# The value products of four attention layers as one product of 1120 columns in three parts a token half

## The chip, the cores and the metric

The kernel runs on one core of a Trainium2 chip. The metric is the device time of one execution in microseconds (us); lower is better. Everything is float32.

## What is computed

Four cross-attention layers follow each other on 128 sequences of 64 tokens and 128 channels. All four read the same context of 64 tokens and 256 channels per sequence. Layer 0 has 16 heads of 64; layers 1 to 3 have 16 query heads of 8 that share 4 key and value heads. Cut to what matters:

```python
# layer 0: x (128, 64, 128), ctx (128, 64, 256)
q = x @ Wq; k = ctx @ Wk; v = ctx @ Wv            # Wv: (256, 1024)
logits = einsum('bhqd,bhkd->bhqk', q, k) * 64 ** -0.5 + col_bias
x = einsum('bhqk,bhkd->bhqd', softmax(logits), v) @ Wo + bo + x
# layers 1 to 3, n_rep = 4
xn = x * rsqrt(mean(x * x) + 1e-5) * norm_w
q = xn @ wq; k = ctx @ wk; v = ctx @ wv           # wv: (256, 32)
scores = einsum('bgrtd,bsgd->bgrts', q, k) / sqrt(8)
x = x + einsum('bgrts,bsgd->btgrd', softmax(scores), v) @ wo
```

The values of all four layers are products of the same context with 1024 + 3 x 32 = 1120 columns of weights.

## The kernel before

**Tiling.** The batch is cut into 32 groups of four sequences (G = 4, so 256 tokens, in two token halves of 128, NP = 2). A group goes through these steps; the names are those of the tables and of the code.

- cT: transpose of the context. k (four units, 256 columns x four blocks): keys of layer 0. v (four units): values of layer 0, unit u for token half u // 2 and column half u % 2, a product of 512 columns with two parts of the contraction. k3: keys of the small layers. v3: values of the small layers, 96 columns for each token half, both in one bank.
- xT: transpose of x, q0 (four units): queries of layer 0. s: scores. add, max, sub, exp, sum, rcp, nrm: the softmax, four units of [128, 512] a layer. t: transposes of the probabilities on TensorE, et: their copy back on ScalarE. pv0, wo0: probabilities times values and the output product of layer 0.
- For layers 1 to 3: xt, q, s, the softmax, t and et, pv, wo, and x2, ssq, ms for the root mean square.

In this text t1.0 is unit 0 of step t of layer 1, v5 is unit 5 of v, and a step without a layer number belongs to layer 0 (t.2, et.0).

**Every float32 product is two instructions** in the trace, each with its own weight load, so a v step of two matmul calls shows as four.

**The order** is written out. Tables (PE_TIME, ACT_TIME, DVE_TIME, POOL_TIME, SP_TIME, lines 38 to 115) give each step a slot for group 0; group g comes PERIOD = 44.42 later. `steps` (L123) sorts the slots, and only the order of the result is used: each engine runs its steps one after the other and waits by semaphore for what a step needs. Steps of several groups so lie interleaved: while group g is at s of layer 0, group g-1 is in layers 1 and 2, group g-2 in layer 3, and keys and values of g+1 and g+2 are made.

**The banks.** PSUM has four banks for scores and four for all else. The latter are dealt in turn, in the order of TensorE's steps (L239 to 246), one to a step, two to pv0, none to s. Before TensorE writes a bank, it waits for the engine that empties the step that held it (L386 to 392): for a t step that is et on ScalarE, for most others ScalarE too, for wo0 and wo VectorE. So a step waits until the step four places before it is emptied.

**Buffers that this touches:** V (three, values of layer 0), VB (five, values of the small layers, laid out in a zeroed 48-column pattern so that one product serves all heads). A v bank is emptied by one copy of 512 columns (L550), the v3 bank by four copies of 64 partitions x 96 (L558).

**The start.** SP's queue issues the loads (L284 to L306): context of groups 0 and 1, Wk and Wv in two halves each, x of group 0, context of group 2, Wq, then per small layer wk, wv, wq, wo and the norm, then bo and Wo. `l_sm` counts the small ones, and its last value is awaited in one go. Ahead of the products of a k step TensorE runs 12 or 13 waits on a semaphore that has long been met (PE_FILL, L403).

Of the kernel before, what the change touches and what calls it, by code (L numbers as in the profile page):

```python
# [29 lines left out]

# [4 lines left out]
PE_FILL = (13, 12, 12, 12)  # L36
PERIOD = 44.42
PE_TIME = {
    "cT": {0: (0,)},
    "k": {0: (87.13, 53.5, 69.79, 100.51)},  # L40
    "v": {0: (76.65, 104.7, 93.39, 95.33)},
    "k3": {0: (106.87,)},
    "v3": {0: (119.52,)},
    "xT": {0: (104.43,)},
    "q0": {0: (127.22, 128.52, 123.66, 130.25)},
    "s": {0: (135.84, 134.86), 1: (170.09,), 2: (201.09,), 3: (235.6,)},
    "t": {0: (152.37, 152.81, 153.25, 154.12),
          1: (185.9, 186.33, 188.92, 181.8),
          2: (216.93, 219.96, 218.23, 218.66),
          3: (256.06, 253.91, 246.56, 247.05)},  # L50
    "pv0": {0: (154.65, 155.64)},
    "wo0": {0: (160.36,)},
    "xt": {1: (164.84,), 2: (196.58,), 3: (228.38,)},
    "q": {1: (167.65,), 2: (198.11,), 3: (232.91,)},
    "pv": {1: (192.23,), 2: (222.65,), 3: (257.89,)},
    "wo": {1: (195.27,), 2: (225.72,), 3: (259.99,)},
}
ACT_TIME = {
    "cT": {0: (1.97,)},
    "k": {0: (89.05, 55.41, 73.19, 105.46)},  # L60
    "v": {0: (79.49, 106.67, 95.3, 97.24)},
    "k3": {0: (107.93,)},
    "v3": {0: (120.61,)},
    "xT": {0: (104.9,)},
    "q0": {0: (128.28, 129.57, 127.42, 131.77)},
    "exp": {0: (146.18, 140.23, 145.62, 141.07),
            1: (177.19, 178.4, 180.19, 174.99),
            2: (210.83, 213.91, 205.74, 205.03),
            3: (247.73, 244.1, 239.23, 240.44)},
    "et": {0: (153.01, 153.5, 153.99, 154.76),  # L70
           1: (186.59, 187.08, 189.55, 182.94),
           2: (217.62, 221.12, 218.92, 220.13),
           3: (256.7, 254.76, 247.24, 248.45)},
    "pv0": {0: (156.34, 157.32)},
    "x2": {1: (169.12,), 2: (200.39,), 3: (226.99,)},
    "xt": {1: (165.63,), 2: (197.14,), 3: (229.63,)},
    "q": {1: (168.84,), 2: (198.9,), 3: (233.61,)},
    "pv": {1: (194.03,), 2: (223.8,), 3: (259.05,)},
}
DVE_TIME = {  # L80
    "add": {0: (140.99, 136.97, 140.1, 136.04)},
    "max": {0: (142.36, 138.07, 141.68, 138.75),
            1: (172.53, 175.26, 173.9, 171.24),
            2: (206.32, 203.59, 202.91, 202.23),
            3: (242.1, 240.75, 236.75, 237.43)},
    "sum": {0: (147.03, 143.03, 146.35, 143.99),
            1: (178.19, 179.29, 183.85, 176.63),
            2: (212.11, 214.8, 210.55, 208.98),
            3: (250.07, 245.23, 241.42, 243.67)},
    "rcp": {0: (149.94, 143.79, 150.14, 145.07),  # L90
            1: (178.95, 181.15, 185.21, 177.99),
            2: (214.49, 216.34, 211.91, 210.35),
            3: (251.42, 246.32, 242.78, 245.03)},
    "wo0": {0: (164.14,)},
    "ssq": {1: (169.66,), 2: (201.49,), 3: (233.51,)},
    "sub": {1: (174.57, 177.3, 175.94, 173.21),
            2: (209.66, 211.22, 204.95, 204.26),
            3: (244.34, 242.98, 238.1, 239.19)},
    "wo": {1: (195.91,), 2: (226.51,), 3: (260.97,)},
}  # L100
POOL_TIME = {
    "xb": {0: (129.82,)},
    "sub": {0: (143.48, 138.82, 142.43, 139.87)},
    "nrm": {0: (150.22, 144.52, 151.26, 145.57),
            1: (179.31, 181.43, 185.49, 178.27),
            2: (214.77, 216.62, 212.19, 210.62),
            3: (251.7, 247.4, 243.05, 245.31)},
    "ms": {1: (173.24,), 2: (201.97,), 3: (235.46,)},
}
SP_TIME = {  # L110
    "cT": {0: (114.98,)},
    "kr": {1: (126.98,), 2: (115.48,), 3: (147.9,)},
    "xT": {0: (215.32,)},
    "st": {0: (292.17,)},
# [4 lines left out]
ON_ACT = ("xT", "q0", "pv0", "xt", "q", "pv", "cT", "k", "v", "v3", "k3")  # L119
# [36 lines left out]
def xattn_kernel(nc, t):  # L156
    with ExitStack() as ctx:
# [16 lines left out]
        wv0 = sb("wv0", [128, 2, 1024])  # L174
# [5 lines left out]
        wvs = sb("wvs", [128, 2, 3, 32])  # L180
# [70 lines left out]
        l_wk, l_wv = ([signal(f"{n}{i}", [i], 16) for i in range(2)] for n in ("l_wk", "l_wv"))  # L251
        l_sm = signal("l_sm", range(17), 16)
# [29 lines left out]
        def sync_program(e):  # L282
# [7 lines left out]
            for i, half in enumerate(halves):  # L290
                e.dma_start(wv0[:, :, half], wv_r[:, :, half]).then_inc(l_wv[i].sem, 16)
# [39 lines left out]
        def gpsimd_program(e):  # L331
# [9 lines left out]
            w.wait_ge(l_sm, 16)  # L341
# [26 lines left out]
        def tensor_program(e):  # L368
# [9 lines left out]
            for st in PE_ORDER:  # L378
# [21 lines left out]
                elif kind == "k":  # L400
                    w.wait_ge(a_ev, ("cT", g, 0, 0))
                    w.wait_ge(l_wk[u // 2], u // 2)
                    for _ in range(PE_FILL[u]):  # L403
                        e.wait_ge(l_ident.sem, 16)
# [6 lines left out]
                elif kind == "v":  # L411
# [346 lines left out]
```

## Time and profile before

| | |
|---|---|
| median of 3 runs | 1492.88 us (1490.64 to 1494.28) |
| profiled execution | time 1492.95 us, span 1491.0 us |
| TensorE busy (products) | 1449.9 us, 97% |
| TensorE busy (weight loads) | 1161.2 us, 78% |
| VectorE busy | 1087.8 us, 73% |
| ScalarE busy | 1038.8 us, 70% |
| GpSimd busy | 774.4 us, 52% |
| mean granted clock of TensorE | 0.987 of 2.4 GHz |

The span is the time from the first to the last instruction; the time of the execution is 1.95 us longer. Busy time of TensorE is from a product's start to its modelled end, and the ends overlap the next start by some 0.16 us; what a step costs TensorE is therefore read as the distance from its start to the start of the next.

### The profile page before, as it was taken

To read this page: it belongs to the slowest core of one execution; us is meant where nothing else is said; L and a number is where in the kernel's file an instruction comes from. 1 tells how busy PE (TensorE), PEld (TensorE's weight loads), DVE (VectorE), ACT (ScalarE), POOL (GpSimd) and SP (SyncE) were. 2 spreads that over 40 slices of the span, in tenths; PEclk is the share of its full clock that TensorE was granted. 3 is DMA by queue.
4 is the path that set the end of the run, shared out by engine and by line. 5 is a ranking of instruction groups with operands and counts; after the bars stand their busy time and mean duration, and the time that the engine had idled before them with its cause. 6 is when DMAs were issued, how large, how long until landed. Compare 5 with 4: busy or idle time off the path is not lost.

```text
span 1491.0 us, 56683 instructions
## 1 busy us (share of the span) xinstructions
PE 1449.9 (97%) x23872; PEld 1161.2 (78%) x23872; DVE 1087.8 (73%) x2291; ACT 1038.8 (70%) x2145; POOL 774.4 (52%) x881
## 2 busy tenths in 40 slices
PE   8999999999999999999999999999999999999875
PEld 5777877887877887877887877887877887877664
DVE  1467777777777877777777777777777777777874
ACT  3566776776776776776777776777776777777663
POOL 3345555545555545555545555545555545555642
PEclk9999999999999999999999999999999999999986
DMA  5010100110000111000110000111000110000000
GB/s 146 21 24 19 26 14 25 27 26 25 22 14 25 27 26 25 21 15 25 26 27 24 22 16 24 26 27 24 22 19 20 26 27 25 15 17 16 15 11 8
DMA packets 57178, 36.94 MB, mean 25 GB/s; under 512 B 16864, under 2 KB 55776, under 8 KB 56928
## 3 DMA queue, kind: packets, MB, share of 16 engines
q1 hardware_dynamic: 56032, 33.22, 8.8%
q8 instruction: 192, 3.15, 0.9%
q14 instruction: 58, 0.48, 0.1%
q10 hardware_dynamic: 896, 0.10, 0.0%
HBM read 16.49 MB, written 4.19 MB: 14 GB/s over the span
## 4 chain that ended last, share of the span: by engine, by line
PE 95%; DVE 2%; ACT 1%; SPq 1%; issue 1%; ACTq 0%; POOL 0%; DMA 0%; POOLq 0%; DVEq 0%
PE bank L408 15%; PE bank L474 15%; PE bank L416 15%; PE bank L492 7%; PE bank L443 7%; PE scores L465 7%; PE bank L511 7%; PE scores L454 4%; PE bank L483 4%; PE bank L517 4%; PE bank L373 3%; PE bank L498 3%; PE bank L424 2%; PE bank L431 2%; SPq L323 1%; DVE st L672 1%
## 5 line engine op out<-in xcount | busy, mean ns | idle before, releaser
L357 POOL TENSOR_TENSOR E<-E,st 128x512 f32<-128x512 f32 x512 | 531.7, 1044 | 609.5 <-DVE st L684 600.2
L681 DVE TENSOR_REDUCE st<-E 128x8 f32<-128x512 f32 x512 | 342.3, 674 | 119.2 <-ACT E L585 64.6
L593 ACT COPY E<-bank 128x512 f32<-128x512 f32 x512 | 290.3, 589 | 30.6 <-PE bank L474 29.6
L474 PEld LDWEIGHTS bank<-ident,E 128*128 128x128 f32 x2048 | 242.4, 143 | 75.1 <-issue 42.8
L672 DVE TENSOR_REDUCE st<-scores 128x8 f32<-128x512 f32 x384 | 254.3, 684 | 63.2 <-PE scores L465 63.2
L474 PE MATMUL bank<-ident,E 128*128 128x128 f32 x2048 | 289.8, 278 | 10.4 <-POOL E L357 10.4
L589 ACT ACTIVATE E<-E,inv 128x512 f32<-128x512 f32 x384 | 277.1, 730 | 23.3 <-DVE E L676 22.4
L676 DVE TENSOR_TENSOR E<-scores,st 128x512 f32<-128x512 f32 x384 | 256.1, 674 | 0.0
L408 PE MATMUL bank<-cT,wk 128*128 128x256 f32 x1024 | 244.8, 383 | 2.1 <-ACT cT L539 1.9
L416 PE MATMUL bank<-wv,cT 128*128 128x512 f32 x512 | 240.5, 593 | 0.0
L408 PEld LDWEIGHTS bank<-cT,wk 128*128 128x128 f32 x1024 | 187.3, 192 | 25.4 <-ACT cT L539 2.3
L353 POOL TENSOR_TENSOR E<-E,st 128x512 f32<-128x512 f32 x128 | 130.9, 1044 | 39.1 <-DVE st L669 39.1
L416 PEld LDWEIGHTS bank<-wv,cT 128*128 128x128 f32 x512 | 87.6, 190 | 62.7 <-issue 62.6
L443 PE MATMUL bank<-xT,wq 128*128 128x256 f32 x512 | 131.0, 380 | 0.0
L511 PEld LDWEIGHTS bank<-E,VB 128*32 128x32 f32 x6144 | 92.7, 112 | 35.7 <-issue 17.4
L492 PEld LDWEIGHTS bank<-wo,QT 128*128 128x128 f32 x1024 | 119.2, 192 | 1.6
L492 PE MATMUL bank<-wo,QT 128*128 128x128 f32 x1024 | 119.5, 275 | 0.0
L580 ACT ACTIVATE QT<-bank 128x512 f32<-128x512 f32 x128 | 77.1, 603 | 57.1 <-PE bank L517 37.2
L662 DVE TENSOR_TENSOR E<-scores,bias 128x512 f32<-128x512 f32 x128 | 86.6, 677 | 40.7 <-PE scores L454 37.1
L511 PE MATMUL bank<-E,VB 128*32 128x64 f32 x6144 | 108.4, 223 | 6.5 <-ACT E L593 6.4
L465 PE MATMUL scores<-KB,QT 32*64 32x256 f32 x3072 | 109.2, 392 | 4.3 <-issue 2.2
L544 ACT COPY KT<-bank 128x512 f32<-128x512 f32 x128 | 74.9, 585 | 46.0 <-PE bank L408 42.0
(62 smaller groups left out, 1689.6 us busy)
## 6 DMA issues: line engine op xcount, KB each, us to landing
KB<-K SPq DMA_DIRECT2D x1536, 8.0 KB
cin<-in_ctx SPq DMA_DIRECT2D x32, 256.0 KB, 2.9
xin<-in_x SPq DMA_DIRECT2D x32, 128.0 KB, 2.5
out<-xN SPq DMA_DIRECT2D x32, 128.0 KB, 1.9
wk<-in_L_xattn_Wk SPq DMA_DIRECT2D x2, 512.0 KB, 7.8
wv<-in_L_xattn_Wv SPq DMA_DIRECT2D x2, 512.0 KB, 9.7
wq<-in_L_xattn_Wq SPq DMA_DIRECT2D x1, 512.0 KB, 9.4
wo<-in_L_xattn_Wo SPq DMA_DIRECT2D x1, 512.0 KB, 5.3
```

Of the source, the lines that this page charges most:

```text
L357: e.tensor_tensor(E3, E3, wide(stat[s][u][:, 16:24]), ALU.mult).then_inc(g_nrm.sem, 1)
L408: m = e.matmul(bank[:, T * jj:T * jj + T], wk0[:, k, 128 * j:128 * j + 128], cTg[:, k, :], start=(k == 0), stop=(k == 1))
L416: m = e.matmul(bank[:, :], cTg[:, k, 128 * p:128 * p + 128], wv0[:, k, 512 * half:512 * half + 512], start=(k == 0), stop=(k == 1))
L443: m = e.matmul(bank[:, T * jj:T * jj + T], wq0[:, 128 * j:128 * j + 128], xT[s][:, :], start=True, stop=True)
L474: m = e.transpose(bank[:, 128 * k:128 * k + 128], E[s][u][:, 128 * k:128 * k + 128], ident[:, :])
L492: m = e.matmul(bank[:, 128 * p:128 * p + 128], QT[s][:, j, 128 * p:128 * p + 128], wo0[:, j, :], start=(j == 0), stop=(j == 7))
L511: m = e.matmul(bank[32 * r:32 * r + 32, 64 * b:64 * b + 64], VBg[:, b, c:c + 32], E[s][2 * (b // 2) + r // 2][:, n:n + 64], start=(gp == 0 ...
L589: e.activation(E[s][u][:, :], E[s][u][:, :], ACT.Exp, scale=inv[s][:, u // 2:u // 2 + 1]).then_inc(a_exp.sem, 1)
L593: e.copy(E[s][u][:, :], bank_of["t", g, l, u][:, :]).then_inc(a_et.sem, 1)
L672: e.tensor_reduce(stat[s][u][:, 0:8].rearrange("p (r h) -> p r h", r=2), scores_of[g, l, u], AX, ALU.max).then_inc(d_max.sem, 1)
L676: e.tensor_tensor(pairs(E[s][u][:, :]), scores_of[g, l, u], stat[s][u][:, 0:8].rearrange("p (r h a) -> p r h a", r=2, a=1).to_broadcast([1 ...
L681: e.tensor_reduce(stat[s][u][:, 8:16], heads(E[s][u][:, :]), AX, ALU.add).then_inc(d_sum.sem, 1)
```

## The change

A new table `VCOLS` cuts the 1120 columns (1024 of layer 0 and 3 x 32) into 374, 374 and 372. The weights lie in one buffer `wv` of 1120 columns. Step v now has six units, unit u for token half u // 3 and column part u % 3; v3 is gone. Parts 0 and 1 are emptied by one copy of 374 columns each. Part 2 is emptied by a copy of the 276 columns that belong to layer 0 and by four copies of 64 partitions x 48 into VB.

The loads of the value weights change: the two parts of 374 columns, then the 276 columns and the three small matrices, all ahead of x of group 0, with a semaphore `l_wvs` of their own. pv0 waits for all three parts of its token half, pv for units 2 and 5. The empty waits ahead of k are left out for group 0. All five tables have new slots, and PERIOD is 44.18.

The core of the diff:

```diff
+VCOLS = ((0, 374), (374, 748), (748, 1120))
-PERIOD = 44.42
+PERIOD = 44.18
 PE_TIME = {
-    "k": {0: (87.13, 53.5, 69.79, 100.51)},
-    "v": {0: (76.65, 104.7, 93.39, 95.33)},
-    "v3": {0: (119.52,)},
-    "s": {0: (135.84, 134.86), 1: (170.09,), 2: (201.09,), 3: (235.6,)},
-          1: (185.9, 186.33, 188.92, 181.8),
-    "q": {1: (167.65,), 2: (198.11,), 3: (232.91,)},
+    "k": {0: (96.87, 67.67, 82.19, 116.05)},
+    "v": {0: (89.47, 99.45, 117.77, 107.38, 105.68, 108.86)},
+    "s": {0: (146.31, 147.29), 1: (180.68,), 2: (213.22,), 3: (246.23,)},
+          1: (198.49, 199.79, 198.93, 193.56),
+    "q": {1: (179.1,), 2: (210.24,), 3: (243.55,)},
 ACT_TIME = {
-    "v": {0: (79.49, 106.67, 95.3, 97.24)},
-    "v3": {0: (120.61,)},
-    "et": ... 1: (186.59, 187.08, 189.55, 182.94),
+    "v": {0: (92.68, 103.53, 119.22, 108.83, 107.13, 110.31)},
+    "et": ... 1: (199.48, 200.76, 200.27, 195.89),
 SP_TIME = {
-    "cT": {0: (114.98,)},
-    "st": {0: (292.17,)},
+    "cT": {0: (104.14,)},
+    "st": {0: (281.38,)},
...
-        wv0 = sb("wv0", [128, 2, 1024])
-        wvs = sb("wvs", [128, 2, 3, 32])
+        wv = sb("wv", [128, 2, 1120])
...
-            for i, half in enumerate(halves):
-                e.dma_start(wv0[:, :, half], wv_r[:, :, half]).then_inc(l_wv[i].sem, 16)
+            for i, (lo, hi) in enumerate(VCOLS[:2]):
+                e.dma_start(wv[:, :, lo:hi], wv_r[:, :, lo:hi]).then_inc(l_wv[i].sem, 16)
+            e.dma_start(wv[:, :, 748:1024], wv_r[:, :, 748:1024]).then_inc(l_wvs.sem, 16)
+            for l in range(3):
+                e.dma_start(wv[:, :, 1024 + 32 * l:1056 + 32 * l], t[f"L{l + 1}_xattn_wv"].rearrange(
+                    "(k p) n -> p k n", p=128)).then_inc(l_wvs.sem, 16)
             e.dma_start(xin[0][:, :, :], x_r[0]).then_inc(l_x[0].sem, 16)
             e.dma_start(cin[2][:, :, :], c_r[2]).then_inc(l_c[2].sem, 16)
...
-                    for _ in range(PE_FILL[u]):
+                    for _ in range(PE_FILL[u] if g else 0):
                         e.wait_ge(l_ident.sem, 16)
...
                 elif kind == "v":
                     w.wait_ge(a_ev, ("cT", g, 0, 0))
-                    p, half = u // 2, u % 2
-                    w.wait_ge(l_wv[half], half)
+                    p, i = u // 3, u % 3
+                    lo, hi = VCOLS[i]
+                    if i < 2:
+                        w.wait_ge(l_wv[i], i)
+                    else:
+                        w.wait_ge(l_wvs, 3)
                     for k in range(2):
-                        m = e.matmul(bank[:, :], cTg[:, k, 128 * p:128 * p + 128],
-                                     wv0[:, k, 512 * half:512 * half + 512], start=(k == 0), stop=(k == 1))
-                    m.then_inc(p_ev.sem, 1)
-                elif kind == "v3":
-                    w.wait_ge(a_ev, ("cT", g, 0, 0))
-                    w.wait_ge(l_sm, 16)
-                    for p in range(NP):
-                        for k in range(2):
-                            m = e.matmul(bank[:, 96 * p:96 * p + 96], cTg[:, k, 128 * p:128 * p + 128],
-                                         wvs[:, k, :, :].rearrange("p l n -> p (l n)"), start=(k == 0), stop=(k == 1))
+                        m = e.matmul(bank[:, 0:hi - lo], cTg[:, k, 128 * p:128 * p + 128], wv[:, k, lo:hi],
+                                     start=(k == 0), stop=(k == 1))
                     m.then_inc(p_ev.sem, 1)
...
                 elif kind == "v":
                     w.wait_ge(p_ev, st)
+                    p, i = u // 3, u % 3
+                    lo, hi = VCOLS[i]
                     if g >= NV:
                         w.wait_ge(p_ev, ("pv0", g - NV, 0, 0), ("pv0", g - NV, 0, 1))
-                    e.copy(V[g % NV][:, u // 2, 512 * (u % 2):512 * (u % 2) + 512], bank[:, :]).then_inc(a_ev.sem, 1)
-                elif kind == "v3":
-                    w.wait_ge(p_ev, st)
-                    w.wait_ge(g_zero, NVB - 1)
-                    if g >= NVB:
-                        w.wait_ge(p_ev, ("pv", g - NVB, 3, 0))
-                    for g2 in range(2):
-                        for b2 in range(2):
-                            m = e.copy(
-                                VB[g % NVB][64 * g2:64 * g2 + 64, :, :].rearrange(
-                                    "q (p b) (i c) -> q p b i c", b=2, c=48)[:, :, b2, :, 8 * g2:8 * g2 + 8],
-                                bank[64 * b2:64 * b2 + 64, 0:96 * NP].rearrange(
-                                    "q (p i g d) -> q p i g d", p=NP, i=6, g=2)[:, :, :, g2, :])
+                    m = e.copy(V[g % NV][:, p, lo:min(hi, 1024)], bank[:, 0:min(hi, 1024) - lo])
+                    if i == 2:
+                        w.wait_ge(g_zero, NVB - 1)
+                        if g >= NVB:
+                            w.wait_ge(p_ev, ("pv", g - NVB, 3, 0))
+                        for g2 in range(2):
+                            for b2 in range(2):
+                                m = e.copy(
+                                    VB[g % NVB][64 * g2:64 * g2 + 64, 2 * p + b2, :].rearrange(
+                                        "q (i c) -> q i c", c=48)[:, :, 8 * g2:8 * g2 + 8],
+                                    bank[64 * b2:64 * b2 + 64, 1024 - lo:1120 - lo].rearrange(
+                                        "q (i g d) -> q i g d", i=6, g=2)[:, :, g2, :])
                     m.then_inc(a_ev.sem, 1)
```

By the slots, the parts of a beat that matter below run in this order on the two engines (the number in brackets is the group, relative to that of s). TensorE, before: s(0), s(0), wo2(-2), t1.3(-1), v2(+1), xt3(-2), v3-unit(+1), t1.0(-1), t1.1(-1), k1(+2). TensorE, after: s(0), s(0), pv2(-2), t1.3(-1), v4(+1), wo2(-2), v3-unit(+1), xt3(-2), v5(+1), t1.0(-1), t1.2(-1), q3(-2), t1.1(-1), k1(+2), s3(-2), and later v2(+1), wo1(-1), t.0(0), k3(+1), xt2(-1), t.1(0), t.2(0). ScalarE, after: v3-unit(+1), exp.0, xt3, v5, et1.0, q3, et1.2, et1.1, exp.1, and later v2, et.0, k3, xt2, et.1. ("v3-unit" is unit 3 of step v.) At the start TensorE's order is cT, cT(1), k1, k2, v0, k0, cT(2) before, and cT, cT(1), k1, k2, cT(2), v0, k0 after.

## Rows read from the trace of the kernel before

**Rows 1.** The page, part 1: busy us (share of the span), instructions.
```profile
span 1491.0 us, 56683 instructions
PE 1449.9 (97%) x23872; PEld 1161.2 (78%) x23872; DVE 1087.8 (73%) x2291; ACT 1038.8 (70%) x2145; POOL 774.4 (52%) x881
```

**Rows 2.** Busy time of each engine in a stretch (window, its length, busy us).
```profile
190.00:1000.00 810.00, 809.94 (x13559) 651.12 (x13558) 615.78 (x1291) 586.96 (x1219) 433.32 (x491) 1.00 0.09 23
```

**Rows 3.** The chain that ended last, in order of time: start us, us, what.
```profile
36.94 1.73 PE bank L408 x8
...
55.00 0.09 issue
55.09 1.97 PE bank L408 x8
...
131.38 2.10 PE bank L483 x128
...
1290.54 2.09 PE bank L483 x128
```

**Rows 4.** TensorE's timeline, 631 to 636 us: start us, us, instruction, count.
```profile
631.10 1.03 PE L424 MATMUL bank<-wvs,cT 128*128 128x96 f32 x8
631.96 0.38 PE L373 MATMUL bank<-ident,xN 128*128 128x128 f32 x2
632.18 0.60 PE L474 MATMUL bank<-ident,E 128*128 128x128 f32 x4
632.62 1.88 PE L416 MATMUL bank<-wv,cT 128*128 128x512 f32 x4
634.34 0.60 PE L474 MATMUL bank<-ident,E 128*128 128x128 f32 x4
634.77 0.60 PE L498 MATMUL bank<-xT,wqs 128*128 128x256 f32 x2
635.21 1.03 PE L443 MATMUL bank<-xT,wq 128*128 128x256 f32 x4
```

**Rows 5.** The same timeline, around two steps "wo", at 638 and 662 us.
```profile
638.25 0.71 PE L517 MATMUL bank<-wos,QT 128*128 128x128 f32 x4
638.79 1.03 PE L443 MATMUL bank<-xT,wq 128*128 128x256 f32 x4
...
662.50 0.61 PE L517 MATMUL bank<-wos,QT 128*128 128x128 f32 x4
662.95 1.03 PE L431 MATMUL bank<-cT,wks 128*96 128x256 f32 x4
```

**Rows 6.** ScalarE's timeline, 632 to 634 us.
```profile
632.16 0.97 ACT L558 COPY VB<-bank 64x96 f32<-64x96 f32 x4 [2.80 <-PE bank L424]
633.16 0.37 ACT L611 COPY xT<-bank 128x256 f32<-128x256 f32 x1
633.43 0.59 ACT L593 COPY E<-bank 128x512 f32<-128x512 f32 x1
```

**Rows 7.** ScalarE's groups by line: busy us, mean ns of one, idle before.
```profile
L550 ACT COPY V<-bank 128x512 f32<-128x512 f32 x128 | 75.1, 587 | 35.6 <-PE bank L416 34.8
L558 ACT COPY VB<-bank 64x96 f32<-64x96 f32 x128 | 29.9, 234 | 87.0 <-PE bank L424 85.9
```

**Rows 8.** Timeline of SP's queue at 6 us.
```profile
6.22 0.53 SPq L293 DMA_DIRECT2D cin<-in_ctx  x1
```

**Rows 9.** The tile cin between 6 and 18 us: its one load.
```profile
DMA to landing us min/median/max: 8.5/8.5/8.5
```

**Rows 10.** TensorE's timeline at the start, 15 to 19 us.
```profile
15.41 1.88 PE L416 MATMUL bank<-wv,cT 128*128 128x512 f32 x4
...
18.86 0.60 PE L373 MATMUL bank<-ident,cin 128*128 128x128 f32 x4
```

**Rows 11.** TensorE's timeline near the end: s of layer 0, last group.
```profile
1398.42 1.26 PE L454 MATMUL scores<-KT,QT 64*64 64x64 f32 x68
```

More of the change, by code:

```diff
@@ L74 @@
[L74 to L78, printed above, removed]
+    "cT": {0: (1.57,)},
+    "k": {0: (99.25, 71.97, 84.11, 117.97)},
+    "v": {0: (92.68, 103.53, 119.22, 108.83, 107.13, 110.31)},
+    "k3": {0: (120.97,)},
+    "xT": {0: (116.66,)},
+    "q0": {0: (142.23, 143.94, 139.53, 140.39)},
+    "exp": {0: (153.41, 157.06, 157.62, 158.18),
+            1: (190.7, 192.3, 185.7, 186.91),
+            2: (225.63, 220.28, 218.71, 224.19),
+            3: (258.05, 259.75, 256.35, 251.03)},
@@ L79 @@
+    "et": {0: (164.29, 165.81, 166.3, 167.12),
+           1: (199.48, 200.76, 200.27, 195.89),
+           2: (235.6, 234.39, 226.6, 233.9),
+           3: (265.32, 267.22, 261.36, 261.85)},
+    "pv0": {0: (168.69, 170.39)},
+    "x2": {1: (179.34,), 2: (211.79,), 3: (240.62,)},
+    "xt": {1: (178.03,), 2: (209.71,), 3: (242.34,)},
+    "q": {1: (179.72,), 2: (210.98,), 3: (244.17,)},
+    "pv": {1: (204.25,), 2: (237.85,), 3: (269.15,)},
 }
 DVE_TIME = {
-    "add": {0: (140.99, 136.97, 140.1, 136.04)},
@@ L82 @@
[L82 to L99, printed above, removed]
+    "add": {0: (148.07, 148.96, 152.37, 153.74)},
+    "max": {0: (149.65, 153.06, 154.43, 156.19),
+            1: (181.83, 188.76, 183.38, 184.26),
+            2: (218.84, 214.36, 216.39, 215.04),
+            3: (252.64, 255.37, 249.96, 247.52)},
@@ new lines @@
+    "sum": {0: (155.52, 157.79, 158.47, 160.02),
+            1: (191.58, 194.52, 187.41, 188.09),
+            2: (226.89, 223.37, 221.8, 225.07),
+            3: (259.9, 261.46, 257.23, 254.7)},
+    "rcp": {0: (156.87, 159.82, 161.39, 162.27),
+            1: (192.95, 196.36, 190.33, 189.44),
+            2: (228.24, 224.47, 223.17, 226.69),
+            3: (261.26, 262.82, 258.32, 256.05)},
+    "wo0": {0: (176.5,)},
+    "ssq": {1: (179.88,), 2: (213.72,), 3: (243.48,)},
+    "sub": {1: (186.72, 189.64, 184.93, 185.62),
+            2: (221.11, 219.51, 217.95, 222.48),
+            3: (254.01, 256.25, 253.32, 249.07)},
@@ L100 @@
+    "wo": {1: (208.04,), 2: (240.14,), 3: (274.68,)},
 }
 POOL_TIME = {
[L102 to L108, printed above, removed]
+    "xb": {0: (147.62,)},
+    "sub": {0: (150.4, 153.81, 155.18, 156.94)},
+    "nrm": {0: (158.99, 160.1, 161.67, 162.71),
+            1: (193.23, 196.64, 190.76, 189.72),
+            2: (228.52, 224.75, 223.44, 226.96),
+            3: (261.53, 263.1, 258.6, 256.32)},
@@ L250, in xattn_kernel @@
         l_wq = signal("l_wq", ["l_wq"], 16)
-        l_wk, l_wv = ([signal(f"{n}{i}", [i], 16) for i in range(2)] for n in ("l_wk", "l_wv"))
-        l_sm = signal("l_sm", range(17), 16)
+        l_wk = [signal(f"l_wk{i}", [i], 16) for i in range(2)]
+        l_wv = [signal(f"l_wv{i}", [i], 16) for i in range(2)]
+        l_wvs = signal("l_wvs", range(4), 16)
+        l_sm = signal("l_sm", range(14), 16)
         l_b = signal("l_b", range(7), 16)
@@ L477, in tensor_program @@
                     w.wait_ge(a_et, ("et", g, 0, 2 * u), ("et", g, 0, 2 * u + 1))
-                    w.wait_ge(a_ev, ("v", g, 0, 2 * u), ("v", g, 0, 2 * u + 1))
+                    w.wait_ge(a_ev, *[("v", g, 0, 3 * u + i) for i in range(3)])
                     for j in range(8):
@@ L537, in scalar_program @@
                     if g >= NC:
-                        w.wait_ge(p_ev, ("v3", g - NC, 0, 0), ("k3", g - NC, 0, 0), *[(k, g - NC, 0, i) for k in "kv" for i in range(4)])
+                        w.wait_ge(p_ev, ("k3", g - NC, 0, 0), *[("k", g - NC, 0, i) for i in range(4)],
+                                  *[("v", g - NC, 0, i) for i in range(6)])
                     e.copy(cT[g % NC][:, :, :].rearrange("p k n -> p (k n)"), bank[:, :]).then_inc(a_ev.sem, 1)
```

53 lines of the change are left out of this document (20 added, 33 removed).

## The prediction

> **What bounds the kernel now.** I read the page first: TensorE is busy 97% of the span [rows 1]. Then the stretches: from 190 to 1000 us it is busy 809.94 of 810 us [rows 2], so in the middle nothing but the sum of its steps counts, and an idle tenth in every group would be paid about 30 times. The chain in order of time gives the beat: product P·V of layer 0 comes at 131.38 us and, 26 groups later, at 1290.54, which is 44.583 us for a group of four batches [rows 3]. ScalarE has room on average (70%), but an average doesn't tell whether one particular copy is in time, and that is what the case turns on.
>
> TensorE's own timeline prices the steps, start to next start [rows 4]. A "v" step (512 columns, four instructions) takes 1.72 us (632.62 to 634.34), so 0.430 an instruction. A "k" step (256 columns, eight instructions) takes 1.73 by the chain (the piece at 36.94) [rows 3], so 0.216. The "v3" step (96 columns, eight instructions) takes 0.86 (631.10 to 631.96), so 0.108: far more than its share by columns (96/512 of 0.430 is 0.081), since each of its instructions brings a new load of 128 weight columns. That is what the change goes for.
>
> **The products.** Before, a group has four v steps and one v3: 4 x 1.72 + 0.86 = 7.74 us, 24 instructions. After, it has six v steps of 374, 374 and 372 columns, again 24 instructions. The trace has none of that width. Between the 256 and the 512 columns of [rows 3, 4] a line gives 0.216 + 118/256 x 0.214 = 0.315 for 374 and 0.313 for 372, so 16 x 0.315 + 8 x 0.313 = 7.54. Gain 0.20 us a group. If the neighbours' rounding is wrong by 2 ns an instruction it is 0.15 to 0.25. The weight load lies under a 0.315 us product as it does under the 0.216 us one. For 32 groups: -6.5 us (-4.8 to -8.0).
>
> **The order around narrow products.** Steps on 32 or 64 rows or columns of the array ("s", "pv", "pv0") form four runs in a group, before and after by the two tables. Leaving such a run costs the next step: "wo" after s1 takes 0.54 (638.25 to 638.79), "wo" after a v step 0.45 (662.50 to 662.95) [rows 5]. In the new order wo2 and wo3 no longer follow a run (-0.18), two "t" steps do instead (nothing to +0.09 each), and a t step rather than cT stands ahead of s0 (nothing to +0.07). Between -0.18 and +0.07; the planner's own slots for these five steps come to -0.04, which lies near the middle, and I take it: -1.3 us in 32 groups (-5.8 to +2.2).
>
> **The copies on ScalarE, and the new wait.** In place of one v3 step whose bank was emptied by four copies of 64 x 96, two steps in a group (v2 and v5, the third part of each token half) must be emptied by one copy of 276 columns and four of 64 x 48. As work this is little: before, 4 x 0.587 + 4 x 0.234 = 3.3 us [rows 7]; after, 4 copies of 374 columns, 2 of 276 and 8 small ones, some 4.2 us; one more in 44. As a delay it is not little. What is seen: a copy of 256 columns lasts 0.37 and the next starts 0.27 after it (633.16, 633.43), so wide copies overlap by 0.10. The four small ones don't: four take 0.97 with 0.234 for one [rows 7], so they start 0.245 apart (one duration and 0.011), and the copy behind them starts at 633.16, 0.03 after their end [rows 6]. A 64 x 48 copy has 48 columns less, at (0.589 - 0.37)/256 = 0.86 ns a column 0.04 us: 0.194, spaced 0.205. The 276-column copy lasts 0.37 + 0.017 = 0.387; I give it no overlap with the small one behind it, as none is seen in the other direction (with overlap 0.10 less). So the bank of v5 is emptied in 0.40 + 3 x 0.205 + 0.194 = 1.21 us. The table of the change sets the next ScalarE step, et1.0, only 0.81 us behind v5.
>
> Who waits: the banks are dealt in turn, four of them. After v5 TensorE runs t1.0, t1.2, q3, t1.1, k1. So t1.1 needs the bank of v5, and k1 the bank of t1.0, which et1.0 empties, and et1.0 stands behind v5's copies in ScalarE's queue. TensorE has t1.0, t1.2, q3 and t1.1 to do before k1: four steps of 0.43 to 0.44 (a t at 632.18, a q at 634.77), 1.74 us [rows 4]. ScalarE's side, from the same instant: 0.20 until its first copy starts (631.96 to 632.16), 1.21 for the bank, 0.03 to the next, 0.59 for et1.0, and about 0.09 until a k step runs after a copy that it waited for (the "issue" piece at 55.00) [rows 3, 6]: 2.12 us. TensorE stands for 0.38 us in every group, some 0.2 of it already ahead of t1.1. With the first copy overlapped it is 0.27; with small copies still 0.245 apart, 0.53. This happens where v5, layer 1's transposes and a further group's k1 all exist, 30 times: +11.4 us (+8 to +16). Queued behind the wait on TensorE are only k1, s3 and all that follows in its order; ScalarE isn't made late by it. The same five copies after v2 fit: xt2, which takes that bank, comes 0.44 + 0.44 + 0.86 = 1.74 later against 0.20 + 1.21 + 0.09 = 1.50, and t.2, which needs et.0's bank, comes 0.22 + 0.44 later still.
>
> The Trainium skill ("ScalarE: Activation LUTs", section "What ACT_TABLE_LOAD costs") says that back-to-back ACTIVATEs overlap by about 93 ns. The wide copies of [rows 6] agree (0.10), the four narrow ones don't. By the page the bank would be free about 0.5 us sooner and the wait would be gone; that is the first rival below.
>
> **The start.** Four transfers of value weights (the 276 columns, and three small ones that stood among the small weights) now go ahead of x of group 0, the context of group 2 and Wq in SP's queue. That context was issued at 6.22 and landed 8.5 later, at 14.7; an issue there costs 0.53 [rows 8, 9], so it lands 0.5 to 2.1 later. The new order wants it two steps sooner: not at 18.86, behind v0 and k0, but at 15.4, right behind the first two k steps [rows 10]. A wait of nothing to 1.5 us; I take 0.8. The rest of the moved transfers is covered: x is wanted some 10 us later. The 12 or 13 empty waits ahead of each k step, gone in group 0, cost at most 0.1. In the first groups the reordered softmax steps of layer 0 are nearer to their consumers; nothing to 2, I take 0.5. In the steady part SP's queue keeps its 48 small copies a group; by the new slots it issues its loads 23 and 28 us ahead of the steps that want them, and the store 28 us ahead: nothing.
>
> **The end.** From s0 of the last group at 1398.42 [rows 11] to 1491 us the chain runs through four layers with TensorE often idle. By both tables the same steps of the two groups before it are left at that point but for pv2, 1 us of TensorE's; the order within DVE's and GpSimd's steps differs. The wait for an old store, which was level with the Wo product there, goes. I put nothing, with 4 either way.
>
> **Sum**, against the profiled execution (span 1491.0, time 1492.95, 0.07 above the median of the runs): -6.5 - 1.3 + 11.4 + 0.8 + 0.5 = +4.9. So 1492.9 + 4.9 = 1497.8 us, and a beat of 44.58 - 0.20 - 0.04 + 0.38 = 44.72.
>
> **Rivals.** (1) The narrow copies overlap after all, or the bank is free earlier for another reason: no wait at t1.1 and k1, the beat is 44.34, and the time 1497.8 - 11.4 = 1486.4, faster. For it: wide copies overlap, and the table was laid out with 0.81 us. Against it: the same kind of copy in the trace takes 0.245 where the old table allowed 0.15, and there the bank was wanted only 2 us later, so that nothing showed. The point from which it decides: v5's bank emptied and et1.0 begun within about 0.86 us. (2) The wait is there at half the size (first copy overlapped and the lag to k1 shorter): 0.2 a group, 6 us, 1492.4, no difference. (3) A column costs more at widths that aren't a power of two, or the wide step does not pay: no gain of 0.20, with the wait, 1504. (4) The new order waits in further places at the start and the end, or for the copies of v2 too: 5 us and more on top, 1503.
>
> **How the numbers follow.** Chances: forecast 0.55, spread by the bounds of the wait over 1494 to 1503; rival 1 0.26; rival 2 0.11; rivals 3 and 4 together 0.08. The range 1485.5 to 1503 takes in rival 1 but for the part of it where the order's gain too is large, and leaves out about 0.15. A measurement tells 0.3%, 4.5 us, from nothing: faster is below 1488.4, slower above 1497.4. Rival 1 is nearly all faster (0.26). Of the forecast 0.35 lies above 1497.4 and of the last two 0.07: slower 0.42. The rest is the same, 0.32.
>
> **What would show it.** In the changed kernel's profile: matmuls of 374 columns spaced 0.315; no step of 96 columns; the beat of P·V at 44.72. TensorE idle 30 times by some 0.2 ahead of a transpose, released by a copy into V or VB, and 30 times by some 0.2 ahead of K, released by a copy into E. ScalarE's five copies lasting 1.2 us in all. A wait for the context near 15 us. Wrong would be: small copies spaced 0.1, a middle without idle time (then 1486), a wait elsewhere, or more than 5 us of difference in the last 90 us.

## Result and the profile after

| | before | after |
|---|---|---|
| median, measured on the same chip | 1491.76 us (4 runs) | 1525.3 us (4 runs, 1517.76 to 1533.28) |
| ratio after / before | | 1.0225, 95% interval 1.0156 to 1.0293 |
| profiled execution | 1492.95 us, span 1491.0 | 1533.28 us, span 1531.4 |

The changed kernel is 33.5 us slower. The forecast was 1497.8 us, at most 1503; the time lies outside that range. The page of after, with its queue of instruction loads:

```profile
span 1531.4 us, 56792 instructions
PE 1464.2 (96%) x23872; PEld 1189.2 (78%) x23872; DVE 1071.4 (70%) x2291; ACT 1077.0 (70%) x2337; POOL 776.7 (51%) x881
...
q8 instruction: 192, 3.15, 0.9%
```

ScalarE has 192 more instructions and 38 us more of work [rows 1]. TensorE's busy time grew by 14 us, though its products should have become shorter. Its waits, summed (engine, line, what it waited for: us in total, times, longest):

```profile
PE bank L485 <- issue: 26.7, 15, 2.4
PE bank L476 <- POOL E L363: 10.7, 8, 6.4
```

L485 is P·V of layer 0 (pv0). In 15 of 32 groups TensorE stops in the middle of this step, and no wait on another engine ends then: "issue" is time in which the profile shows nothing that it waited for. The wait on GpSimd is that of the last groups, where before has 10.4 us of the same. One such stop in the timeline (start, us, instruction, count), and the windows around it (length, then busy us of PE, PEld, DVE, ACT and POOL, the granted clock, DMA share, GB/s):

```profile
133.41 1.59 PE L485 MATMUL bank<-E,V 64*64 64x64 f32 x90
137.12 1.10 PE L485 MATMUL bank<-E,V 64*64 64x64 f32 x38 [2.12 <-issue]
138.15 2.01 PE L467 MATMUL scores<-KB,QT 32*64 32x256 f32 x32
```

```profile
134.00:137.00 3.00, 1.00 (x66) 0.86 (x57) 1.49 (x4) 2.59 (x6) 1.63 (x2) 1.00 0.09 18
137.10:141.00 3.90, 3.88 (x75) 2.70 (x76) 0.74 (x2) 1.69 (x3) 1.03 (x3) 0.56 0.07 15
141.00:145.00 4.00, 4.00 (x30) 3.75 (x30) 4.00 (x9) 2.13 (x4) 1.85 (x2) 1.00 0.06 12
```

After 90 of 128 products nothing runs for 2.12 us. Behind it the granted clock is 0.56: TensorE falls to the lower of its two levels, 1.2 GHz, for most of 3.9 us, and step s that follows takes 2.01 us for the usual 1.05. Such a beat is 48.6 to 48.8 us long, and there are four. Of the eight stops of 2.1 us and more a fifth, ending at 1376.06, is followed by 0.56 as well, but lies in the last groups, where beats are shorter. The other three leave the clock at 1.00, and their beats are 46.6 to 47.1.

Where no stop falls, the kernel does what was forecast. The same stretch as [rows 4], TensorE and then ScalarE:

```profile
629.83 1.42 PE L426 MATMUL bank<-wv,cT 128*128 128x372 f32 x4
631.09 1.04 PE L476 MATMUL bank<-ident,E 128*128 128x128 f32 x8
631.96 0.60 PE L500 MATMUL bank<-xT,wqs 128*128 128x256 f32 x2
632.43 0.66 PE L476 MATMUL bank<-ident,E 128*128 128x128 f32 x4
633.07 1.97 PE L414 MATMUL bank<-cT,wk 128*128 128x256 f32 x8
634.97 1.12 PE L467 MATMUL scores<-KB,QT 32*64 32x256 f32 x32
```

```profile
631.29 0.39 ACT L555 COPY V<-bank 128x276 f32<-128x276 f32 x1 [0.21 <-PE bank L426]
631.57 0.81 ACT L562 COPY VB<-bank 64x48 f32<-64x48 f32 x4
632.40 0.58 ACT L597 COPY E<-bank 128x512 f32<-128x512 f32 x1
```

v5 takes 1.26 us (629.83 to 631.09). The five copies end at 632.38, and t1.1, which needs their bank, comes only 0.05 later, at 632.43; et1.0 ends at 632.98, and k1 comes at 633.07. The products carry no bracket for these waits, since modelled ends overlap the next start. In the distances they are seen: from q3 to t1.1 it is 0.47 for a usual 0.43, from t1.1 to k1 0.64 for 0.44, k1 takes 1.90 for 1.82. The weight loads, which come just ahead of the products, do show them, summed over the run (engine, line, what it waited for: us in total, times, longest):

```profile
PEld bank L476 <- ACT VB L562: 8.0, 29, 0.3
PEld bank L414 <- ACT E L597: 5.6, 28, 0.2
```

These are the two signs that the prediction had named: some 0.2 to 0.3 us behind a copy into VB, and 0.2 behind a copy into E, in nearly every group. The beat of this group is 44.71 us, pv0 at 599.62 to pv0 at 644.33.

**Where the 40.4 us between the two spans lie.** pv0 of group 2 comes 2.0 us later than in before (133.41, 131.38). From there to pv0 of the last group it is 1323.4 us instead of 1284.7: 38.7 more. The rest is 0.4 shorter. Of the 38.7 some 3.8 are the longer beat of clean groups (29 x 0.13), 26.7 the stops, and some 9 the half clock behind five of them (beats of 48.6 against 46.8, so 1.8 each). The three make 39.5; before has a stop of 1.37 us in the same stretch, near 1401, so they account for 38.1.

### The profile page after: what moved, and what is told of

It is laid out like the page before. It is cut to its first block, busy times and chain, and to the rows that moved or that the text cites. A ratio compares the mean times of both kernels' runs of the same rounds, so it can differ in the third digit from the quotient of the medians.

```text
span 1531.4 us, 56792 instructions
## 1 busy us (share of the span) xinstructions
PE 1464.2 (96%) x23872; PEld 1189.2 (78%) x23872; DVE 1071.4 (70%) x2291; ACT 1077.0 (70%) x2337; POOL 776.7 (51%) x881
## 3 DMA queue, kind: packets, MB, share of 16 engines
q8 instruction: 192, 3.15, 0.9%
## 4 chain that ended last, share of the span: by engine, by line
PE 93%; DVE 3%; issue 2%; ACT 1%; SPq 1%; DMA 0%; POOL 0%
PE bank L426 16%; PE bank L476 15%; PE bank L414 15%; PE bank L445 7%; PE bank L494 7%; PE scores L467 7%; PE bank L513 7%; PE bank L485 5%; PE scores L456 4%; PE bank L379 3%; PE bank L519 3%; PE bank L500 3%; PE bank L433 2%; DVE st L676 1%; DVE E L680 1%
## 5 line engine op out<-in xcount | busy, mean ns | idle before, releaser
L685 DVE TENSOR_REDUCE st<-E 128x8 f32<-128x512 f32 x512 | 336.3, 667 | 153.4 <-ACT E L593 99.4
L476 PE MATMUL bank<-ident,E 128*128 128x128 f32 x2048 | 301.1, 282 | 10.9 <-POOL E L363 10.7
L476 PEld LDWEIGHTS bank<-ident,E 128*128 128x128 f32 x2048 | 239.1, 144 | 76.0 <-POOL E L363 24.6
L426 PE MATMUL bank<-wv,cT 128*128 128x374 f32 (+1 forms) x768 | 271.5, 477 | 0.0
L414 PE MATMUL bank<-cT,wk 128*128 128x256 f32 x1024 | 248.7, 386 | 1.3 <-ACT cT L542 1.0
L426 PEld LDWEIGHTS bank<-wv,cT 128*128 128x128 f32 x768 | 136.5, 190 | 52.5
L555 ACT COPY V<-bank 128x374 f32<-128x374 f32 (+1 forms) x192 | 86.0, 448 | 74.8 <-PE bank L426 73.4
L445 PE MATMUL bank<-xT,wq 128*128 128x256 f32 x512 | 125.8, 380 | 0.0
L699 DVE TENSOR_TENSOR xN<-bank,xN 128x256 f32<-128x256 f32 x96 | 40.3, 420 | 120.6 <-PE bank L519 120.6
L467 PE MATMUL scores<-KB,QT 32*64 32x256 f32 x3072 | 113.1, 402 | 4.9 <-issue 2.6
```

What stands on the lines that cost most here:

```text
L414: m = e.matmul(bank[:, T * jj:T * jj + T], wk0[:, k, 128 * j:128 * j + 128], cTg[:, k, :], start=(k == 0), stop=(k == 1))
L426: m = e.matmul(bank[:, 0:hi - lo], cTg[:, k, 128 * p:128 * p + 128], wv[:, k, lo:hi], start=(k == 0), stop=(k == 1))
L445: m = e.matmul(bank[:, T * jj:T * jj + T], wq0[:, 128 * j:128 * j + 128], xT[s][:, :], start=True, stop=True)
L476: m = e.transpose(bank[:, 128 * k:128 * k + 128], E[s][u][:, 128 * k:128 * k + 128], ident[:, :])
L685: e.tensor_reduce(stat[s][u][:, 8:16], heads(E[s][u][:, :]), AX, ALU.add).then_inc(d_sum.sem, 1)
```

## Experiments

Three questions: what causes the stops, whether the wait behind the five copies is real and of the forecast size, and whether another order does better. In this part the *place* of an instruction is its number in TensorE's program, modulo 256. In both kernels a group has exactly 1536 instructions, six pieces, so from group 3 on each step keeps its place. pv0 stands at 19 in before and at 13 in after.

### The empty waits

```diff
-                    for _ in range(PE_FILL[u] if g else 0):
+                    for _ in range(PE_FILL[u]):
```

> The changed kernel with one line of the change undone: the empty waits ahead of each k step run in group 0 too, which puts 25 more instructions ahead of everything that follows on TensorE and changes nothing else. Theory A (the 16 standstills of some 2 us inside pv0 are instructions that come late, and come late because of where in the 16 KB pieces of the instruction stream pv0 lies, at place 13 of 256): they go or move, the beat is 44.71 in all groups, time about 1496. Theory B (they come from the new order or the wider products themselves, whatever the place): they stay, time 1515 to 1533. If both places are bad, pv0 (now 38) and s0 (now 36) stand still elsewhere, and the text of A has to say so.

Measured: 1497.65 us (1496.39 to 1499.41), ratio 1.0041 [1.0026, 1.0055]. The stops in pv0 are gone but for two, in group 1 and in group 30, 3.4 us together; the beat is 44.62, in some groups 44.72 to 44.82. One line that adds 25 instructions to group 0 is worth 27.7 us. pv0 now stands at 38.

The other way round, the same line in the kernel before:

```diff
-                    for _ in range(PE_FILL[u]):
+                    for _ in range(PE_FILL[u] if g else 0):
```

> The kernel before with only the one line of the change that leaves the empty waits out in group 0: 25 instructions less, pv0 at place 250 instead of 19, s0 at 131 instead of 156. Theory A: standstills may appear somewhere, 1495 to 1530, with the beat 44.58 where there is none. Theory B: nothing happens, 1492.

1492.67 us, ratio 1.0002 [0.9993, 1.0012], beat 44.58. The waits in group 0 have no use of their own, and the old order bears this shift. Is place 13 for pv0 bad in itself? The kernel before with `PE_FILL[u] if g or u != 1 else 0` has pv0 there:

> The kernel before with 6 instructions less on TensorE in group 0: pv0 at place 13, where the changed kernel has it, all else as before (s0 at 150). Theory A in its simple form (the place of pv0 decides): standstills in pv0, 1505 to 1530. Theory B: 1492.

1491.59 us, ratio 0.9997 [0.9987, 1.0007]. It isn't. And the changed kernel with pv0 at the place that it has in before, 19 (`PE_FILL[u] if g else (12 if u == 1 else 0)`):

> The changed kernel with 6 more instructions on TensorE in group 0 (12 empty waits ahead of its k1), so that pv0 lies at place 19 of a piece in the steady part, exactly where it lies in the kernel before, and s0 at 17. Theory A: if the place of pv0 alone decides, no standstill, 1496. If what counts is how the place meets the waits ahead of pv0, standstills may stay: 1510 to 1530. Theory B: 1515 to 1533.

1532.93 us, ratio 1.0273 [1.0240, 1.0307], 15 stops of 27.6 us. So place 19 serves the old order and not the new one. The remaining question was whether e1 helps by the place or by slowing the start. 50 empty waits ahead of k1 of group 0 alone (`50 if u == 1`), 25 instructions in one spot:

> The changed kernel with 50 empty waits ahead of k1 of group 0 alone, 25 instructions: pv0 and s0 at places 38 and 36 as in e1, but not spread over four k steps. Place alone: like e1, 1497 to 1499. If it counts that the waits stand ahead of each k step of group 0, the standstills are back, 1515 to 1533.

1499.95 us, ratio 1.0047 [1.0032, 1.0062], beat 44.62, and no stop in pv0 between groups 2 and 29. The count decides, not which steps have the waits.

### Half a piece further

256 empty waits, 128 instructions, ahead of k1 of group 0, in the new order (`256 if u == 1 else 0`) and in the old one (`PE_FILL[u] + (0 if g or u != 1 else 256)`):

> The changed kernel with 256 empty waits ahead of k1 of group 0, which are 128 instructions: pv0 at place 141 and s0 at 139, half a piece further. Theory A (the place decides): no standstill in pv0 or s0 at this place, beat 44.6 to 44.7, 1498 and at most 1 more for the waits. If instead half a piece is bad as well, standstills in other steps, over 1510. Theory B (leaving out the waits is bad for another reason than place): since waits are there again, this tells nothing against A.

> The kernel before with 256 further empty waits ahead of k1 of group 0, 128 instructions: pv0 at place 147 and s0 at 28. If the old order too has places at which instructions come late, standstills in pv, s or s0 and 1500 to 1590 (e7 gave 1589 for the new order at such a place). If the old order is safe everywhere (it was at 250, 13 and 19), 1493 to 1505, some 13 at most for the piece that the waits themselves want at the start.

1589.47 us, ratio 1.0648 [1.0622, 1.0674], and 1559.32 us, ratio 1.0446 [1.0428, 1.0465]. So the old order isn't immune. The stops lie in other steps now; waits of the two kernels:

```profile
PE bank L513 <- issue: 39.8, 29, 2.6
PE scores L467 <- issue: 18.2, 32, 1.2
PE bank L414 <- issue: 12.8, 1, 12.8
```

```profile
PE scores L465 <- issue: 19.2, 31, 1.2
PE scores L454 <- issue: 13.9, 26, 1.2
PE bank L408 <- issue: 13.5, 1, 13.5
```

Then the better variant (below) with the waits of group 0 doubled, pv0 at 62:

```diff
-                    for _ in range(PE_FILL[u]):
+                    for _ in range(PE_FILL[u] * (1 if g else 2)):
```

> As e13 with twice as many empty waits in group 0, so 24 more instructions: pv0 at place 62, s0 at 60. If only places just behind the start of a piece are bad, as e13. e7 at 141 was bad, so somewhere between 38 and 141 the standstills in pv and s begin: if at 62 already, over 1500.

1513.93 us, ratio 1.0139 [1.0125, 1.0153], 27 stops in t. One stop of each of the three kernels (new order, old order, e15):

```profile
882.25 2.10 PE L456 MATMUL scores<-KT,QT 64*64 64x64 f32 x128
884.28 0.63 PE L513 MATMUL bank<-E,VB 128*32 128x64 f32 x27
886.12 0.76 PE L513 MATMUL bank<-E,VB 128*32 128x64 f32 x37 [1.21 <-issue]
```

```profile
840.91 2.10 PE L483 MATMUL bank<-E,V 64*64 64x64 f32 x128
842.93 1.09 PE L465 MATMUL scores<-KB,QT 32*64 32x256 f32 x22
844.49 0.67 PE L465 MATMUL scores<-KB,QT 32*64 32x256 f32 x10 [0.47 <-issue]
```

```profile
841.76 2.10 PE L456 MATMUL scores<-KT,QT 64*64 64x64 f32 x128
843.79 1.10 PE L513 MATMUL bank<-E,VB 128*32 128x64 f32 x64
846.17 0.38 PE L476 MATMUL bank<-ident,E 128*128 128x128 f32 x2 [0.92 <-issue]
```

Counted in places, the stops tell one thing. In after, in e2, e6, e14, e7, e12 and e15, 212 of the 215 stops of groups 2 to 29 come at one place of 256 or the one next to it, in five different steps. In after: pv0 at 13, 90 products of two instructions each, and a wait, 13 + 180 + 1 = 194. So a stop sits where one piece of 256 ends and the next begins. In the three kernels just shown it is a special piece: the one before it ends inside s0 or pv0, and this one is all narrow products. From 882.68 (27 products into s0) to the stop at 884.91 are 2.2 us; 2.8 in e12, 2.4 in e15. In an ordinary group of before the shortest piece lasts 5.9 us, in e3 5.2, in e1 4.7, and none of them is followed by a stop. A piece that TensorE runs through in under 3 us is followed by one in 135 of 138 cases.

The Trainium skill ("Advanced Engine Details and Errata", section "ISA Cache") says that instructions are cached in lines of 16 KB, 256 instructions, and that there are only two, though it also gives the size for TensorE as 128 KB, which would be eight. The 16 KB agree with the 192 loads of 3.15 MB, the 256 with the stops' places. The traces fit two: in groups 2 to 29 of all 17 kernels no load starts earlier than 1.9 us before TensorE begins the piece ahead of the one that is loaded, so no more than one piece is fetched ahead. Then a short piece leaves its successor's load too little time.

That doesn't explain the stops of after. There the piece that ends inside pv0 lasted 7.3 us. What differs from before is when the load of the next piece starts, by the times of the instruction queue's transfers in the trace. Paired in order, one load to each border of two pieces, they give one rule for all 17 kernels: the 212 stops end 0.9 to 1.6 us after their piece's load has ended (1.4 in the middle), and at the 2644 borders without a stop that load had ended 1.06 us or more before TensorE came, at all but four of them 1.3 or more. So what TensorE waits for is its instructions. In before the load for the piece that begins inside pv0 starts 0.6 to 1.3 us after TensorE has begun the piece ahead of it, and 6.1 us or more before it is wanted. In after it starts 4.4 to 4.9 us after, which is just in time, and in the 14 groups that stop 5.7 to 7.0 us after. One group of each kind: with pv0 at 554.91 the load runs from 553.55 to 554.92, TensorE comes to the border at 556.25, no stop; with pv0 at 509.07 it runs from 508.91 to 510.11, TensorE comes at 510.65 and stands until 511.48. Two causes for a late load were tried.

### Small transfers, late copies

48 small copies K to KB a group share the DMA queues with the instruction loads. e14 is the changed kernel without them from group 2 on: `elif kind == "kr" and g < 2`, and scores of layers 1 to 3 use the keys of groups 0 and 1 (it leaves out the keys of all later groups). Two more empty waits ahead of one k step in each group from 4 on make up for a wait that goes with them, and hold the steps' places.

> The changed kernel (no empty waits in group 0, pv0 at place 13 or 14) without the 48 small copies of keys from K3 to KB from group 2 on; the scores of layers 1 to 3 are then made with old keys. Theory T1 (the piece of the instruction stream comes late because SP's small copies hold the DMA engines): standstills gone or a third of them, 1500 to 1505. Theory T2 (the piece is asked for late; the DMA traffic is not the reason): some 15 standstills as before, 1515 to 1530.

1531.71 us, ratio 1.026 [1.0246, 1.0274], 25 stops of 24.9 us in pv0. Not the transfers. e6 takes three of the four 64 x 48 copies out of the changed kernel, so that ScalarE is early (its edit is that of e5, below):

> The changed kernel as it is (no empty waits in group 0), with one of the four 64 x 48 copies as in e5; three quarters of the small layers' values are left out. Theory A1 (an instruction piece comes late because TensorE's sequencer is held back by the late copies of v2 and v5, at a bad place of pv0): standstills gone, 1486. Theory A2 (the place alone, with the new order, whatever ScalarE does): some 15 standstills stay, beat between them 44.3, time 1510 to 1520.

1514.39 us, ratio 1.0169 [1.0138, 1.0200]: 25 stops of 21.9 us. More stops than in after, and shorter ones; the beats are 44.4 clean and mostly 45.2 to 45.8. ScalarE's lateness doesn't cause them. In both kernels the load ahead of a stop is late as in after (4.8 to 7.0 us into the piece). What makes it late in the new order stays open.

### The five copies

e1 with one of the four small copies; three quarters of the small layers' values are left out:

```diff
-                        for g2 in range(2):
-                            for b2 in range(2):
+                        for g2 in range(1):
+                            for b2 in range(1):
```

> As e1 (empty waits of group 0 back), but the banks of v2 and v5 are emptied by the 276-column copy and one of the four 64 x 48 copies; three quarters of the small layers' values are left out. TensorE's instructions are the same to the last. The prediction's wait: the bank of v5 is free 0.6 us sooner, TensorE no longer stands ahead of t1.1, k1 and k3-unit; beat 44.62 - 0.38 = 44.24 (at least 44.34), time 1497.7 - 11 = 1486. Rival (the beat is what the products and the order cost, the wait is not there): beat stays 44.62, 1497.

1487.19 us (1483.34 to 1488.5), ratio 0.9965 [0.9953, 0.9977], beat 44.30 in every steady group, 0.32 below e1. The waits ahead of t1.1 and k1 are gone, and so are the two rows of waits of the weight loads:

```profile
652.26 0.60 PE L500 MATMUL bank<-xT,wqs 128*128 128x256 f32 x2
652.69 0.60 PE L476 MATMUL bank<-ident,E 128*128 128x128 f32 x4
653.13 1.89 PE L414 MATMUL bank<-cT,wk 128*128 128x256 f32 x8
654.95 0.90 PE L467 MATMUL scores<-KB,QT 32*64 32x256 f32 x24
```

0.43, 0.44 and 1.82 us where e1 has 0.48, 0.64 and 1.89: 0.05 + 0.20 + 0.07 is the whole 0.32. Can it be had with all the copies in? First v4 and v5 changed places, so that the narrow copies come earlier:

```diff
-    "v": {0: (89.47, 99.45, 117.77, 107.38, 105.68, 108.86)},
+    "v": {0: (89.47, 99.45, 117.77, 107.38, 108.86, 105.68)},
```

> As e1 (empty waits of group 0 back), with the slots of v4 and v5 exchanged on TensorE and ScalarE, so that the unit with the five copies comes first of the three and wo2, v3-unit and xt2-like steps lie between it and the next need of its bank. Nothing is left out. The prediction's wait: without it the beat is that of e5, 44.30, time 1487 to 1488, faster than the kernel before by 0.3%. Rival (the copies as work, not their place, cost the 0.32): beat 44.5 to 44.6, 1495.

1495.8 us, ratio 1.002 [1.0011, 1.003], beat 44.61. The wait has moved:

```profile
609.87 1.42 PE L426 MATMUL bank<-wv,cT 128*128 128x374 f32 x4
611.39 0.44 PE L379 MATMUL bank<-ident,xN 128*128 128x128 f32 x2
611.66 1.11 PE L426 MATMUL bank<-wv,cT 128*128 128x374 f32 x3
```

The step behind the v3-unit starts after 1.52 us, not 1.26: it waits for the bank of t1.3, whose copy et1.3 now queues behind the five (610.75 to 611.33). The weight loads of that line wait 19.9 us in 29 groups for a copy into E. So et1.3 was put ahead of them on ScalarE, on top of e9:

```diff
-            1: (199.48, 200.76, 200.27, 195.89),
+            1: (199.48, 200.76, 200.27, 194.4),
```

> As e9 (v4 and v5 exchanged, empty waits back), and et1.3 moved ahead of v5 in ScalarE's order. In e9's trace xt3 now stands 0.3 us late; its bank is that of t1.3, whose copy was behind the five copies of v5. If the prediction's mechanism is right (what stands behind the five copies in ScalarE's queue holds a bank), nothing that is wanted soon is behind them now: beat 44.30, time 1487.5. If the wait only moves once more, beat 44.5 to 44.62, 1495.

1490.59 us (1489.05 to 1493.32), ratio 0.9981 [0.9972, 0.9991]: 0.2% below before, with nothing left out; the interval leaves out 1, but the gain is 2 to 3 us and not the 5 to 6 that were expected. The beat is 44.45 to 44.49, not the expected 44.30. One more wait has come up behind the one removed: xT to the k3-unit takes 0.49 us, where e5 has 0.32.

```profile
660.33 0.44 PE L379 MATMUL bank<-ident,xin 128*128 128x128 f32 x2
660.82 0.45 PE L414 MATMUL bank<-cT,wk 128*128 128x256 f32 x1
```

### The old order with six units

The old tables with a sixth slot for v in place of v3, PERIOD 44.42, waits as in e1:

```diff
+    "v": {0: (76.65, 104.7, 115.9, 93.39, 95.33, 119.52)},       # TensorE
+    "v": {0: (79.49, 106.67, 118.2, 95.3, 97.24, 120.61)},       # ScalarE
```

> The wide product without the new tables: all slots of the kernel before (44.42), v in six units of 374, 374 and 372 columns; v5 takes the slot of v3, v2 stands between k2 and wo0, where ScalarE has 3 us to spare; the empty waits of group 0 are kept. pv0 lies at place 21. The prediction's term for the products alone is -0.20 a group: beat 44.38, time 1492.8 - 6.5 + 0.5 = 1486.8. If wide products bring nothing, 1493; if the copies of v2 and v5 are late here too, beat above 44.45.

1494.93 us, ratio 1.0024 [1.0013, 1.0034], beat 44.61 where 44.38 was expected. The 0.46 us that a v step became shorter had been cover:

```profile
660.83 1.42 PE L426 MATMUL bank<-wv,cT 128*128 128x374 f32 x4
662.22 0.71 PE L519 MATMUL bank<-wos,QT 128*128 128x128 f32 x4
```

```profile
661.56 0.60 ACT L547 COPY KT<-bank 128x512 f32<-128x512 f32 x1
```

wo1 comes 1.39 us behind v1, as it waits for the bank of the k3-unit, which ScalarE empties until 662.16. With the k3-unit and v1 exchanged, so that more of TensorE's work lies between the k3-unit and wo1 (PE_FILL now 13, 12, 12, 10):

```diff
-    "k": {0: (87.13, 53.5, 69.79, 100.51)},    "v": {0: (76.65, 104.7, ...
+    "k": {0: (87.13, 53.5, 69.79, 104.7)},     "v": {0: (76.65, 100.51, ...
```

> As e8 (slots of before, six units), with k3-unit and v1 exchanged: the trace of e8 shows wo1 0.13 us late behind the shorter v1, waiting for the bank of k3-unit, and dearer by 0.10 as the first step behind the wait. With the 1.73 us k3-unit in front of wo1 and v1 emptied early, the cover is back: beat 44.38, time 1487. If s3, now 0.47 sooner behind the step before it, waits instead, beat 44.5 to 44.6, 1493.

1493.31 us, ratio 1.0006 [0.9997, 1.0015], beat 44.55: no difference from before. xT now has 0.11 us of the same kind of wait.

## Why the prediction was wrong, point by point

**The step that failed** is the sentence on the start: "The 12 or 13 empty waits ahead of each k step, gone in group 0, cost at most 0.1". I priced them as time of TensorE, and by e3 that was right. They are also 25 instructions, and their going moved every later step against the pieces in which instructions are loaded. What stands in its place is a wait for instructions, 26.7 us in 15 stops inside pv0, and the lower clock behind five of them. In this order that costs 27.7 us (1525.3 against 1497.65 of e1, which differs in that line alone). The count of instruction loads stood on the page of before, and its trace had "issue" gaps inside narrow steps, 1.37 us in s0 near 1401 us and 1.58 at 92 us. I read them as noise of start and end. No rival had the mechanism either, so nothing in the range did.

**What holds of the sum** holds for e1, the changed kernel without the stops. The sum is 1497.8 us, e1 measured 1497.65, but the agreement is partly luck. By the spans, e1 stands 4.6 us above before (forecast 4.9): 3.0 up to pv0 of group 2, 2.5 from there to the last pv0, less 0.9 at the end. The forecast had 1.3, 3.6 and 0 for these. Near the end of the 2.5 lies a stop of 1.85 us, which no term had; before has one of 1.37 there. Term by term:

- *The products*, 0.315 us an instruction and 1.26 a step: 1.26 measured. Right, and rival 3 is out.
- *The order*: forecast beat without any wait 44.34, e5 has 44.30, so the order brought 0.08, not 0.04. Inside its bounds.
- *The wait behind v5*: forecast 0.38 at t1.1 and k1, measured 0.32 by e1 and e5, at t1.1 0.25 (with q3 ahead of it) and at k1 0.07. The four small copies took 0.81 us, as forecast; the 276-column copy overlapped the first of them by 0.11, which I had not granted it. With that overlap my own sum gave 0.27, so 0.32 lies between my two values. In after another 0.10 falls at the k3-unit (637.05 to 637.46, 0.41 us against 0.31 in e1), so its clean beat of 44.71 meets the forecast 44.72 by a place that I hadn't named. Rivals 1 and 2 are out: e5 shows what rival 1 would have been, 1487.2 us against my 1486.4.
- *The overlap of copies*: the 0.093 us that the Trainium skill ("ScalarE: Activation LUTs", section "What ACT_TABLE_LOAD costs") states for back-to-back ACTIVATEs agree with the 0.11 between the wide copy and the first small one. Not with the small ones among themselves: 0.193 us each by the groups by line and four in 0.81, so 0.205 apart.
- *The start*: the wait for the context of group 2 was forecast at 0.8 us, at most 1.5, and measured 1.72, in e1 2.31.

```profile
14.98 0.66 PE L379 MATMUL bank<-ident,cin 128*128 128x128 f32 x4 [1.72 <-DMA cin<-in_ctx]
```

  By the starts of pv0, e1 is 0.8 us behind before in group 0, 1.8 in group 1 and 3.0 in group 2, against the 1.3 of the forecast. Too low: the wait was mis-sized, and what the 2.2 us of groups 1 and 2 are made of is open. The "issue" stop of 1.59 us in group 1 isn't among them, as before has one of 1.58.
- *The end*: nothing forecast, 0.4 less in after and 0.9 less in e1. Inside the bounds.

That the copies after v2 fit was right: no wait is seen behind them. That the weight load lies under a 374-column product was right too.

## What to carry to other kernels

Where TensorE is busy 97% of the time, its instruction stream is a resource of its own. Instructions that look idle can hold the stream in place, so removing or adding any of them is a change for every later step, and a new order is to be tried at several shifts before it is judged (e1 and after differ by 27.7 us). Count the loads of the instruction queue, find which steps their borders fall into, and keep a piece from being all narrow products, 128 of them. And a step that becomes shorter takes cover away from a copy beside it: in three of these kernels (e8, e9, e13) the gain went to a wait one or two steps further on, found by the distances between starts and the waits of the weight loads, as the products show no idle time for it.

## What the runs showed of the hardware

- TensorE's instructions come in pieces of 16 KB. At a piece's end it can stand still for 0.2 to 2.6 us, once each 12.8 (e7) and 13.5 (e12) in a run of 128 instructions of empty waits at the start. The stop ends 0.9 to 1.6 us after the load of the next piece has ended (212 stops, seven kernels). The same program shifted by 25 instructions ran 1.8% faster, and by another 103 it ran 6.1% slower.
- A stop of 2.12 us inside dense narrow products can be followed by a granted clock of 0.56 over 3.9 us, in which step s takes 2.01 us for 1.05. It isn't always: of two stops of 2.12 us in neighbouring groups (ending at 185.69 and 232.74) only the second is. In after none of the shorter ones (0.56 to 1.86) is, but one of 1.85 us in e1 is (0.66 over the 3.9 us from 1385.43), and one of 2.59 us in e7 isn't. What decides it stays open.
- Four copies of 64 partitions x 48 columns take 0.81 us, 0.205 apart, hardly less than the 0.245 of 64 x 96.
